# Differential attention: the causal mask moved from matrix products on TensorE to an in-place addition on VectorE

## The reference, cut to what matters

```
    def _L0_attn_ref(X, Wq, Wk, Wv, Wo, lq1, lk1, lq2, lk2, rms_scale):
...
        Q, K, V = (proj(Wq), proj(Wk), proj(Wv))
        Q1, Q2 = jnp.split(Q, 2, axis=-1)
        K1, K2 = jnp.split(K, 2, axis=-1)
        lam = jnp.exp(jnp.sum(lq1 * lk1, axis=-1)) - jnp.exp(jnp.sum(lq2 * lk2, axis=-1)) + LAMBDA_INIT
        lam = lam[None, :, None, None]
        scaling = 1.0 / np.sqrt(dh)
        causal = jnp.tril(jnp.ones((n, n), bool))
        A1 = jnp.where(causal, jnp.einsum('bhnd,bhmd->bhnm', Q1, K1) * scaling, -jnp.inf)
        A2 = jnp.where(causal, jnp.einsum('bhnd,bhmd->bhnm', Q2, K2) * scaling, -jnp.inf)
        attn = jax.nn.softmax(A1, axis=-1) - lam * jax.nn.softmax(A2, axis=-1)
        O = jnp.einsum('bhnm,bhmd->bhnd', attn, V)
        rms = jnp.sqrt(jnp.mean(O * O, axis=-1, keepdims=True) + EPS)
        O = O / rms * rms_scale * (1.0 - LAMBDA_INIT)
        Oc = O.transpose(0, 2, 1, 3).reshape(b, n, H * 2 * dh)
        return Oc @ Wo.T
```

## Time and profile before

| | before |
|---|---|
| median of 3 executions | 4580.32 us |
| the profiled execution | 4579.85 us, span 4577.9 us |
| TensorE products (PE) busy | 3809.7 us, 83% |
| TensorE weight loads (PEld) busy | 2311.2 us, 50% |
| VectorE (DVE) busy | 2339.9 us, 51% |
| ScalarE (ACT) busy | 1788.3 us, 39% |
| GpSimd (POOL) busy | 1566.2 us, 34% |
| mean granted clock of TensorE | 0.914 |

### The profile page before, as it was taken

How to read it: one execution, slowest core, us unless ns; L and a number is a source line. 1 busy time by engine, 2 the same in 40 slices (tenths; PEclk the granted TensorE clock), 3 DMA queues, 4 the chain that set the end, 5 groups by cost and what they waited for, 6 DMA issues and landing times. The chain is left out here.

```text
span 4577.9 us, 64482 instructions
## 1 busy us (share of the span) xinstructions
PE 3809.7 (83%) x18416; PEld 2311.2 (50%) x18416; DVE 2339.9 (51%) x5270; ACT 1788.3 (39%) x4038; POOL 1566.2 (34%) x1711
## 2 busy tenths in 40 slices
PE   6999999999589996996999868758999999549950
PEld 4666666666355554543555534334555555336630
DVE  3666666666355552224556423226566555245556
ACT  2544444445245553112555511114555554204420
POOL 2333333433466661003666500021322221262234
PEclk8999999999799998998999979878999999759975
DMA  6555565555110112342011111112222211149952
GB/s 94 70 74 69 76 85 76 75 70 72 59 38 32 37 41 94 151 166 91 24 46 46 37 62 38 53 55 67 62 57 58 56 48 39 41 161 314 322 173 76
DMA packets 245793, 378.22 MB, mean 83 GB/s; under 512 B 55278, under 2 KB 182322, under 8 KB 239154
## 3 DMA queue, kind: packets, MB, share of 16 engines
q1 hardware_dynamic: 232114, 355.35, 32.8%
q0 software_dynamic: 6144, 16.79, 1.1%
q10 hardware_dynamic: 7296, 3.22, 0.3%
HBM read 170.25 MB, written 84.93 MB: 56 GB/s over the span
## 5 line engine op out<-in xcount | busy, mean ns | idle before, releaser
L766 DVE TENSOR_REDUCE a_neg_max<-a_ps 128x1 f32<-128x384 f32 (+3 forms) x768 | 438.4, 596 | 279.2 <-PE a_ps L508 250.6
L2509 DVE TENSOR_REDUCE c_neg_max<-c_ps 128x1 f32<-128x512 f32 x512 | 340.9, 684 | 242.4 <-PE c_ps L2155 240.7
L2348 ACT ACTIVATE c_probsT<-c_ps 128x512 f32<-128x512 f32 x512 | 299.2, 598 | 391.6 <-PE c_ps L2167 382.9
L367 POOL TENSOR_SCALAR_AFFINE_SELECT a_probs_c<-a_probs_c 128x256 f32<-128x256 f32 (+1 forms) x384 | 185.7, 494 | 717.4 <-ACT a_probs_c L654 717.4
L654 ACT ACTIVATE a_probs_c<-a_ps 128x512 f32<-128x512 f32 x640 | 355.1, 600 | 126.1 <-PE a_ps L524 98.3
L1123 PE MATMUL w_ps_e<-w_wqkv,w_hT 128*128 128x512 f32 x768 | 368.9, 605 | 15.8 <-ACT w_hT L1262 8.0
L1061 POOL TENSOR_TENSOR w_probs<-w_probs,w_inv 128x1024 f32<-128x1024 f32 x128 | 242.3, 1893 | 369.7 <-DVE w_inv L1419 369.7
L505 PE MATMUL a_ps<-a_packed_qk 65*128 65x128 f32 (+3 forms) x1024 | 330.2, 365 | 28.4 <-DVE a_neg_max L766 14.7
L542 PE MATMUL a_ps<-a_probs_c,a_v 128*64 128x512 f32 (+3 forms) x2048 | 321.0, 458 | 0.8 <-POOL a_probs_c L367 0.8
L524 PE MATMUL a_ps<-a_packed_qk 67*128 67x512 f32 (+3 forms) x1024 | 293.8, 349 | 0.8 <-DMA a_packed_qk<-a_max_half 0.8
L2155 PE MATMUL c_ps<-c_packed_qk 68*128 68x512 f32 x512 | 260.5, 513 | 4.8 <-DVE c_neg_max L2509 2.5
(11 more groups left out here) (317 smaller groups left out, 7785.4 us busy)
## 6 DMA issues: line engine op xcount, KB each, us to landing
a_packed_qk<-a_halves SPq DMA_DIRECT2D x512, 128.0 KB, 4.6
d_w<-in_L_ffn_second SPq DMA_DIRECT2D x71, 516.0 KB, 5.0
d_w<-in_L_ffn_first SPq DMA_DIRECT2D x71, 512.0 KB, 5.1
rows_dram<-f_zeros SPq DMA_DIRECT2D x8, 4096.0 KB, 15.3
c_packed_qk<-c_halves SPq DMA_DIRECT2D x256, 128.0 KB, 2.3
w_v<-w_v_next SPq DMA_DIRECT2D x16, 1024.0 KB, 4.5
d_rows<-rows_dram SPq DMA_DIRECT2D x71, 128.0 KB, 4.3
mixed_dram<-d_y SPq DMA_DIRECT2D x71, 128.0 KB
```

The source lines that it names most:

```text
L766: nc.vector.tensor_reduce(neg_max[:, hd // 2 % 2, hd % 2, maps[0]:maps[-1] + 1, i], bank("s", (hd, k))[:, 0:len(maps) * keys].rearrange("p ...
L2348: nc.scalar.activation(probsT[:, q % 2, r, :], ps_again[u % 2][:, :], ACT.Exp).then_inc(exp_done.sem, 1)
L2509: nc.vector.tensor_reduce(neg_max[:, g % 2, 0, s % GS:s % GS + 1], bank("s", s)[:, :], AX.X, ALU.max, negate=True).then_inc(max_ready.sem, 1)
```

## The change

The mask product on TensorE is taken out of `scores`; each product of a unit now stands alone. `maxima` waits for the scores in a wait of its own and then does, for each map of the unit, one `tensor_tensor_reduce`: it adds a mask to the scores in PSUM, writes the sum back in place, and gives the maximum over the row. The mask tile is 512 columns wide, 384 zeros and then the 128 causal columns, and a unit of query block i takes its last (i + 1) x 128 columns. The maxima are no longer negated; the transposing product takes a negated identity in its place. Two casts in the setup fall away, one scaling and one memset on POOL come in.

```
-        ident_r = sb("ident_r", [P, P], fp32r)
-        ident = sb("ident", [P, P])
-        causal_r = sb("causal_r", [P, P], fp32r)
+        ident, neg_ident = sb("ident", [P, P]), sb("neg_ident", [P, P])
+
+        mask = sb("mask", [P, NT * P])
...
-        neg_max = sb("neg_max", [P, 2, 2, M, NT])
+        maxima_of = sb("maxima", [P, 2, 2, M, NT])
...
-            loads.extend([(ident[:, :], con["ident"]), (causal_in, con["causal_wide"])])
+            loads.extend([(ident[:, :], con["ident"]), (mask[:, (NT - 1) * P:], con["causal_wide"])])
...
             nc.gpsimd.memset(v[:, :, :, HV:HV + 1], 1.0)
+            nc.gpsimd.memset(mask[:, 0:(NT - 1) * P], 0.0)
             nc.gpsimd.memset(neg_half[:, :, :], -0.5).then_inc(half_made.sem, 1)
...
                 for n, m in enumerate(maps):
-                    nc.tensor.matmul(out[:, n * keys:(n + 1) * keys], packed_qk[0:K_ALL + 1, 0, slot, m, i * P:(i + 1) * P],
-                                     packed_qk[0:K_ALL + 1, 1, slot, m, 0:keys], start=n == 0, stop=False)
-                blocks = out[:, 0:len(maps) * keys].rearrange("p (m n) -> p m n", n=keys)[:, :, i * P:keys]
-                nc.tensor.matmul(blocks, ident_r[:, :], causal_r[:, :].unsqueeze(1).to_broadcast([P, len(maps), P]),
-                                 start=False, stop=True).then_inc(scores_ready.sem, 1)
+                    last = nc.tensor.matmul(out[:, n * keys:(n + 1) * keys],
+                                            packed_qk[0:K_ALL + 1, 0, slot, m, i * P:(i + 1) * P],
+                                            packed_qk[0:K_ALL + 1, 1, slot, m, 0:keys], start=True, stop=True)
+                last.then_inc(scores_ready.sem, 1)
...
-                nc.tensor.matmul(bank("m", p)[0:2 * M * NT, 0:P], neg_max[:, p % 2, :, :, :], ident[:, :],
+                nc.tensor.matmul(bank("m", p)[0:2 * M * NT, 0:P], maxima_of[:, p % 2, :, :, :], neg_ident[:, :],
                                  start=True, stop=True).then_inc(max_psum.sem, 1)
...
             dve.wait_ge(weights_in.sem, 16 * len(loads))
+            dve.wait_ge(half_made.sem, 1)
...
-            nc.vector.tensor_copy(ident_r[:, :], ident[:, :])
-            nc.vector.tensor_copy(causal_r[:, :], causal_in).then_inc(rounded.sem, 1)
+            nc.vector.tensor_scalar(neg_ident[:, :], ident[:, :], -1.0, None, ALU.mult).then_inc(rounded.sem, 1)
...
             def maxima(b, hd, k, live):
                 i, maps = UNITS_S[k]
                 u, keys = US * hd + k, (i + 1) * P
-                dve.wait_ge(scores_ready.sem, scores_ready.at(b, u + 1))
                 if hd % 2 == 0 and k == 0:
                     before = earlier(b, hd, 4, live)
                     if before is not None:
                         dve.wait_ge(max_psum.sem, max_psum.at(before[0], before[1] // 2 + 1))
-                nc.vector.tensor_reduce(neg_max[:, hd // 2 % 2, hd % 2, maps[0]:maps[-1] + 1, i],
-                                        bank("s", (hd, k))[:, 0:len(maps) * keys].rearrange("p (m n) -> p m n", n=keys),
-                                        AX.X, ALU.max, negate=True).then_inc(max_ready.sem, 1)
+                standing_wait(dve, scores_ready.sem, scores_ready.at(b, u + 1), passed_dve.sem)
+                for n, m in enumerate(maps):
+                    tile = bank("s", (hd, k))[:, n * keys:(n + 1) * keys]
+                    last = nc.vector.tensor_tensor_reduce(tile, tile, mask[:, (NT - 1 - i) * P:], 1.0, -3e38, ALU.add, ALU.max,
+                                                          accum_out=maxima_of[:, hd // 2 % 2, hd % 2, m, i:i + 1])
+                last.then_inc(max_ready.sem, 1)
```

More of the change, by code:

```diff
@@ L198, in differential_attention @@
         lam_in = y[:, :, :]
-        causal_in = hT[:, 0, 0:P]
         lam_pr = oT[:, 0, :].rearrange("p (n d) -> p n d", n=2)
@@ L242, in differential_attention @@
         setup_order, rounded = signal("setup_order"), signal("rounded")
-        passed, passed_pool = signal("passed", 0), signal("passed_pool", 0)
+        passed, passed_pool, passed_dve = signal("passed", 0), signal("passed_pool", 0), signal("passed_dve", 0)
         combined = signal("combined", 3 * H)
```

## The result

The changed kernel takes 4571.37 us (median of 20 executions, 4558.32 to 4580.90); the kernel before took 4579.88 beside it (20 executions). The ratio is 0.9979, interval 0.9971 to 0.9988: 8.5 us faster, where 43 had been forecast.

The account below looks back on a forecast made before the run. TensorE was taken to bound the attention stage. Eight batches and loop edges gave -50 us, the start +2, steps with statistics or splits +5: -43, from 4579.85 to 4537 us (forecast 4515 to 4560; full range 4492 to 4640).

Parts of the forecast that it names:

- Steps 9 to 15: Attention steps with projections of this batch and the next: TensorE still bounds at 66.8 us for 71.50, -4.7 a batch.
- VectorE's part: Eight two-input instructions replace six reduces a head: 0.16 us for two more instructions, 1.04 for accumulator reads, 1.20 in sum.
- Steps 4 and 5: Two attention steps of a batch: VectorE's busy time is not near the span, so -1.3 us.
- Step 0: Attention step at the loop's edge: three masks lie behind the wait there, the others ahead of it, -0.3 us.
- The light steps: Steps 1 to 3 and 6 to 8, without projections: VectorE becomes the bound, 38.4 us against 38.26, no gain.
- the read of the accumulator: On VectorE, after each new instruction: between nothing and 0.20 us, taken as 0.13; eight a head make 1.04 us.
- rival A: The accumulator costs nearly nothing; VectorE gets 0.16 us a head and stays under TensorE everywhere: 4496 us, chance 0.15.
- The mask product: Six mask products a head leave TensorE: 0.67 us a head, 86 us over 128 heads; lower end 0.43, 55 us.
- The standing wait: Wait for scores on VectorE: nothing to about 0.1 us each, once or twice a head; within 0.25 us a light step.
- Late next: Next waits: unit 5's maximum in light steps holds the next head's unit 2; unit 0's in even steps holds transposed maxima.
- B: VectorE's columns take twice as long, 3.81 us a head more in sum: 4740 us; chance 0.28 with its milder form.
- C: No change: accumulator reads of 0.20 us and waits of 0.5 us a light step lose 35 us: 4575, chance 0.12.

Follow-up runs that it names:

- doubled: The kernel before with each mask product made twice, so the mask is added twice: 4646.69 us, ratio 1.0164.
- wait and split: The kernel before without mask products or mask addend, with a standing wait and eight plain reduces a head, one per map, for six: 4543.11 us, ratio 0.9927.
- the late change: The changed kernel with head norms and statistics moved on VectorE behind the maxima of unit 5: 4535.54 us, ratio 0.9918 to the kernel before.

## Why the prediction was wrong

*Sign and rough place of the parts:* TensorE was the bound and lost work, VectorE had room for its part; the sign was right. The 8.5 us are a fifth of the 43.

*The step that failed* is the first of the sum: "Steps 9 to 15: TensorE 71.50 - 7 x 0.67 = 66.8 us; VectorE 44.47 + 7 x 1.20 = 52.9. TensorE still bounds, -4.7." It compares busy sums over seven steps. The run without mask products tests it with VectorE's part untouched: over the six batches of the loop these steps gave 2.45 us a batch, not 4.7. That is (4.7 - 2.45) x 8 = 18 of the 43 us, missing before VectorE cost anything. Two things are in it. The price was too high: in batch 4, at a clock of 1.00 in both, TensorE's busy time falls by 3.5 us, 0.51 a head for 0.67. And its idle time grows, from 3.06 us a batch to 4.70.

TensorE was idle 3.2 of the 71.5 us in batch 4 even before. 1.34 us of that is the gap at the loop's edge, where the profile shows nothing that it waits for. Most of the rest are single deliveries of VectorE: 1.5 us for maxima (1.09 of it in step 11) and 0.2 for low halves. Without mask products these are 1.8 at the edge, 1.9 for maxima and 1.4 for low halves. Such a delivery comes at its own time, and a TensorE that arrives earlier waits longer. For the low halves VectorE is not the only one late: it stands still ahead of them itself, for ScalarE's high half (134.8 us over the kernel).

With VectorE's part these steps gave 0.1 us: the idle time is 5.91 us a batch, and five batches of six instead of one lie at a clock of 0.98. The forecast had taken off 5 us in all for steps with statistics or splits, and nothing for the clock. Steps 4 and 5, put at -1.3, gave 0.2 (0.6 without VectorE's part). Step 0, put at -0.3, gave 1.9 in batch 4 and 1.0 in the mean of six.

*The light steps,* forecast at no gain, gained 0.46 us each in steps 1 to 3, nearly in full (a length unchanged within 3% had been named as a sign that the forecast is right; it fell by 7%), but 0.13 together in steps 6 to 8, which have statistics between units 4 and 5. VectorE's part was mis-sized: some 0.4 us a head for 1.20. The term in it that was wrong is the read of the accumulator, put at 0.13 us. It is an instruction of its own of 141 ns, but it runs beside the next one. On the queue the fused instruction takes 0.01 to 0.05 us more than a plain reduce, read and write included, which makes the lower end of that term (rival A) nearly right. The Trainium skill ("VectorE: DVE Perf Modes", "Two Vector instructions with no wait between them") says that such an op is two instructions; the trace agrees, with 1024 reads for 1024 streams. It is where a count of instructions and a price part.

*The mask product* was priced at 0.67 us a head and is worth 0.50 (light steps) to 0.6 (doubled), inside the bounds of 0.43 and 0.67. In steps 9 to 15, 7 x 0.17 us too much is 1.2 a batch, some 9 us in all.

*The standing wait,* at 0.25 us a light step, did no harm in the light steps. On the kernel before it costs 8 us in all, inside the range taken.

*Late next:* "in light steps the maximum of unit 5 [...], in even steps the maximum of unit 0, for which the transposed maxima wait". Both waits came, but as losses in the heavy steps and at the loop's edge, where no price had been put on them. Of the 27.3 us of waits for maxima in the change 22.8 are behind unit 5's; unit 0's are the 35.3 that appeared when the first was bought out. Where TensorE waits, it also goes on later after a fused maximum: 0.11 us behind the end of the stream (686.20 above), where a plain reduce was followed at 0.06. What it waits for is the read, which ends 0.06 us after the stream. There the read does have a price, 0.06 us a wait. The run without mask products, with wait and split, shows the plain case in its step 11 (679.33 less 678.58 + 0.69), VectorE first, then TensorE:

```profile
678.58 0.69 DVE L765 TENSOR_REDUCE a_neg_max<-a_ps 128x1 f32<-128x512 f32 x1
...
679.33 0.44 PE L505 MATMUL a_ps<-a_packed_qk 65*128 65x128 f32 x2 [1.14 <-DVE a_neg_max L765]
```

*The rivals.* A (the accumulator nearly free) had VectorE's part nearly right (0.16 us a head for 0.4) and its time, 4496, wrong, by the same failed step. B did not come: the distance of 512 columns is 0.61 to 0.65 us, not twice the stream. The page "Vector Engine (DVE) Microarchitecture Reference" of the Trainium skill ("Points that are easy to get wrong") speaks of half the throughput for two non-bf16 sources in SBUF; here one is in PSUM, and the halving is not seen. C had the nearest time, 4575, by luck: it came from reads of 0.20 us and longer light steps, and neither happened.

*The range* (4492 to 4640) held the result; it had been drawn for A and B and says nothing in favour of the sum.

## What to carry to other kernels

Busy time by stretch says which engine has more work, not what a saving on it is worth: a heavy stretch with 4% of idle time already waits on single deliveries, and a part of what is saved there turns into longer waits. Look at the same stretch in every batch, with its clock, before reading a difference of a few us from one. Before forecasting, follow the waits of the bound engine instruction by instruction in the heavy steps, and ask which delivery it would meet next if it came earlier. A saving whose gain does not appear may be waiting for the order around it: two moves on the critical deliveries (statistics behind the last maximum, transposes behind the long products) made this change worth 36 to 41 us instead of 8.5. If unmasked maxima are acceptable (the shift is then no smaller than the true maximum, and where a masked score is much larger, the exponentials may underflow), no mask at all is better still: 4497.63 us, the fastest kernel of this study.

## What was not expected of the hardware

The read of the accumulator (141 ns) starts together with the instruction after it, so it costs little on VectorE's queue; the engine that waits for the maximum sees it (0.11 us behind the stream's end for 0.06). When the stream goes to SBUF, both are shorter (708 and 141 ns in place), as the groups by form of the change with its output in SBUF show:

```profile
L768 DVE CUSTOM_DVE_ANT_0 a_masked_out<-a_ps,a_mask 128x512 f32<-128x512 f32 x256 | 170.2, 686 | 0.2
...
L768 DVE DVE_READ_ACCUMULATOR2_ANT a_maxima<- 128x1 f32 x1024 | 84.9, 83 | 0.0
```

And a gap can be followed by a stretch at the lower of the clock's two levels (1.2 GHz of 2.4). Besides step 11 above, step 0 shows it. In batch 4 of the changed kernel TensorE waits 2.55 us there for unit 0's maxima, at a mean granted clock of 0.69 over the step, and the products with V behind it take 4.12 us, where they took 2.37 in step 1 of the kernel before. The kernel before has the same at its own step 0: a wait of 2.97 us, then 4.54. With the transposes behind the products with V, batch 4 has no such wait. They take 3.70, still in part at the lower level, and the step is 8.00 us long instead of 10.88 (the late change: 11.36). In three other batches of that kernel a wait of 0.8 to 2.2 us for something the profile doesn't name stands ahead of them. The order of time on TensorE in the changed kernel:

```profile
595.07 0.61 PE L547 MATMUL a_ps<-a_neg_ident,a_maxima 128*16 128x128 f32 x2 [2.55 <-DVE a_maxima L767]
595.61 4.12 PE L541 MATMUL a_ps<-a_probs_c,a_v 128*64 128x512 f32 x16
```
